# Local attention's output projection as three matmuls of split operands, with single buffers for two middle tiles

## The reference

```python
def attn_layer(x, Wqkv, qs, ksc, Wo):          # 16 heads of 64, INNER = 1024
    q, k, v = jnp.split(x @ Wqkv, 3, -1)        # x has its second half of channels shifted by a row
    q, k = rotary(l2norm(q) * qs), rotary(l2norm(k) * ksc)
    out = local_attention(q, k, v)              # windows of 64 rows, each looks at itself and the one before
    return out.transpose(0, 2, 1, 3).reshape(b, n, INNER) @ Wo
def ffn_layer(x, g, bln, W1, b1, W2, b2):
    a, gate = jnp.split(layer_norm(x) @ W1 + b1, 2, -1)
    return a * gelu(gate) @ W2 + b2
```

## Time and profile before

| | us |
|---|---|
| median of 3 runs | 2143.72 |
| range of the runs | 2138.83 to 2144.59 |
| profiled execution | 2145.24 |
| its span, first to last instruction | 2143.4 |
| PE / DVE / ACT / POOL busy | 2040.7 / 1723.7 / 1392.7 / 550.3 |

### The profile page before, as it was taken

One profiled execution on the slowest core, in us unless ns is written; L12 is line 12 of the kernel. 1 busy time (PEld: TensorE's weight loads), 2 busy tenths in 40 slices (PEclk: granted clock), 3 DMA queues, 4 the chain that ended last, 5 costly groups with the idle time before them and its releaser, 6 DMA issues.

```text
span 2143.4 us, 51804 instructions
## 1 busy us (share of the span) xinstructions
PE 2040.7 (95%) x17400; PEld 1704.1 (80%) x17400; DVE 1723.7 (80%) x4874; ACT 1392.7 (65%) x4026; POOL 550.3 (26%) x317
## 2 busy tenths in 40 slices
PE   5999999999998998999999999999999999999988
PEld 4787887887886676888888888888888888888877
DVE  6786787787676498898889888898889888988883
ACT  3776567567564355676767676866777676767653
POOL 2111111111111334232323233232323242323220
PEclk9999999999999999999999999999999999999999
DMA  3000000000000410021102011201120111011010
GB/s 120 8 10 1 7 12 1 7 12 1 6 26 0 140 31 15 13 72 33 56 14 72 14 58 31 72 14 46 44 73 14 34 57 52 25 33 55 14 33 20
DMA packets 50017, 72.10 MB, mean 34 GB/s; under 512 B 9429, under 2 KB 36869, under 8 KB 49541
## 3 DMA queue, kind: packets, MB, share of 16 engines
q1 hardware_dynamic: 47429, 64.30, 9.9%
q10 hardware_dynamic: 2368, 4.98, 0.6%
HBM read 51.58 MB, written 2.10 MB: 25 GB/s over the span
## 4 chain that ended last, share of the span: by engine, by line
PE 47%; issue 7%; DVE 4%; DMA 3%; ACT 3%; POOL 2%; SPq 1%; DVEq 0%; ACTq 0%; POOLq 0%
PE ps_loc L1722 17%; PE ps_loc L1830 7%; PE ps_loc L1799 5%; PE ps_loc L1761 4%; PE ps_loc L1841 4%; PE ps_loc L1772 4%; DMA late<-y_all 3%; PE ps_loc L1741 3%; PE ps_loc L1788 3%; POOL rnorm L2655 2%; PE ps_loc L1342 1%; ACT xnT_high L2077 1%; ACT pT L2060 1%; ACT xnT_loc L2077 1%; DVE w_low L2259 0%
## 5 line engine op out<-in xcount | busy, mean ns | idle before, releaser
L2655 POOL TENSOR_TENSOR rnorm<-norm_floor,half_loc 128x32 f32<-128x32 f32 x48 | 300.5, 6261 | 582.7 <-DVE norm_floor L2270 385.2
L1722 PE MATMUL ps_loc<-w_high,xT 128*128 128x512 f32 x1152 | 379.3, 410 | 0.7 <-ACT qk L2032 0.6
L2053 ACT ACTIVATE prob_loc<-prob_loc,top_loc 128x128 f32<-128x128 f32 x768 | 299.2, 402 | 45.2 <-DVE top_loc L2334 43.2
L718 ACT ACTIVATE prob<-prob,new_top 128x256 f32<-128x256 f32 x512 | 252.2, 497 | 0.0
L1722 PEld LDWEIGHTS ps_loc<-w_high,xT 128*128 128x128 f32 x1152 | 203.9, 189 | 51.4 <-issue 9.3
L2334 DVE CUSTOM_DVE_ANT_0 prob_loc<-ps_loc,const,rnorm 128x128 f32<-128x128 f32 x768 | 218.8, 345 | 28.0 <-PE ps_loc L1761 25.8
L1722 PE MATMUL ps_loc<-w_low,xT 128*128 128x512 f32 x576 | 228.5, 397 | 0.0
L2045 ACT ACTIVATE qT_loc<-ps_loc 128x512 f32<-128x512 f32 x96 | 57.4, 598 | 238.1 <-PE ps_loc L1741 238.1
L923 DVE CUSTOM_DVE_ANT_0 prob<-ps_cross,bias 128x256 f32<-128x256 f32 x512 | 184.7, 420 | 20.7 <-PE ps_cross L494 11.1
L1799 PE MATMUL ps_loc<-wo,qT_loc 128*128 128x256 f32 x768 | 169.8, 379 | 1.3 <-ACT qT_loc L2067 1.3
L1179 POOL TENSOR_TENSOR o<-o,alpha 128x1024 f32<-128x1024 f32 x32 | 61.0, 1906 | 425.1 <-DVE o L962 333.4
(11 more groups left out here) (214 smaller groups left out, 4869.0 us busy)
## 6 DMA issues: line engine op xcount, KB each, us to landing
w_raw<-in_ffn_Wqkv_dram SPq DMA_DIRECT2D x24, 512.0 KB, 5.7
w_raw<-in_ffn_Wqkv_dram SPq DMA_DIRECT2D x24, 256.0 KB, 3.9
wo<-in_ffn_Wo_dram SPq DMA_DIRECT2D x24, 256.0 KB, 3.5
v_mid<-v_even SPq DMA_DIRECT2D x24, 256.0 KB, 3.4
v_mid<-v_odd SPq DMA_DIRECT2D x24, 256.0 KB, 3.7
w<-in_ffn_W_dram SPq DMA_DIRECT2D x12, 341.0 KB, 3.3
w<-in_ffn_W_dram SPq DMA_DIRECT2D x6, 640.0 KB, 4.6
ctx_raw<-in_ctx_dram SPq DMA_DIRECT2D x12, 256.0 KB, 2.8
```

The source lines that it names most:

```text
L718: ins = act.activation(prob[:, t, h, :], prob[:, t, h, :], ACT.Exp, bias=new_top[:, t, h:h + 1], scale=-1.0, accum_out=chunk_sum[:, t, h:h ...
L1722: ins = pe.matmul(ps[:, DENSE + j % 2, :], xT[:, px, kk, t * P:(t + 1) * P], wqkv[pw][:, kk, col:col + 512], start=kk == 0 and n == 0, sto ...
L2053: ins = act.activation(pr, pr, ACT.Exp, bias=top[:, h, t:t + 1], scale=-1.0, accum_out=total[:, h, t:t + 1])
L2655: pool.tensor_tensor(rnorm[:, b % 2, t, :], norm2_floor[:, :], half[:, :], ALU.pow).then_inc(rnorm_done, 8)
```

## The change

Both operands of the projection are split into a high and a low part. ACT now writes all four groups of `oT_high`, DVE subtracts to get `oT_low` (`o_low`), and PE sums three products. Wo is split too: in slot 0 of each layer, ACT copies the high part right behind `q_out` (`out_weights_high`), and POOL subtracts the low one. Space comes from three places: `oT_low` lies over four of the six pairs of the probabilities' ring (so the next slot's third pair of scores waits for `y_full`), `v_mid` has one buffer, filled once the slot before has used it up, and `late` has one. In DVE's slot, `gated` 4 and 5 now stand ahead of the cosines.

```diff
-        self.wo = self.sb("wo", [P, PAIRS, D])
+        with ExitStack() as shared:
+            self.wo = self.sb("wo", [P, PAIRS, D], F32, shared)
+        self.wo_low = self.sb("wo_low", [P, PAIRS, D], F32R)
+        self.wo_high = self.sb("wo_high", [P, PAIRS, D], F32R)
...
+    LOW_RING = RING - PAIRS // 2
-        v_mid = sb("v_mid", [P, 2, INNER])
+        v_mid = sb("v_mid", [P, INNER])
-        late = sb("late", [P, B * TT, P])
+        late = sb("late", [P, TT, P])
...
             def shift(L, b):
                 sp.wait_ge(y_mid, L + U * (b + 1))
+                hold(sp, k.held)
+                sp.wait_ge(xn_done, L + U * b)
...
             def middle(L, b):
                 sp.wait_ge(qkv_done, L + U * (b + 1))
+                hold(sp, k.held)
+                sp.wait_ge(o_full, L + U * b)
...
             def project_out(a, b):
                 if b == 0:
-                    pe.wait_ge(wo_in, a + LAYER)
+                    pe.wait_ge(wo_split_low, a + LAYER)
                 pe.wait_ge(s_read, a + U)
                 pe.wait_ge(o_done, a + U)
                 for t in range(TT):
-                    for pair in range(PAIRS):
-                        ins = pe.matmul(ps[:, WIDE_OUT, t * D:(t + 1) * D], oT[:, pair, t * P:(t + 1) * P], wo[:, pair, :],
-                                        start=pair == 0, stop=pair == PAIRS - 1)
+                    for n, (po, pw) in enumerate(WIDE_PARTS):
+                        for pair in range(PAIRS):
+                            ins = pe.matmul(ps[:, WIDE_OUT, t * D:(t + 1) * D], oT[po][:, pair, t * P:(t + 1) * P],
+                                            wo_parts[pw][:, pair, :], start=n + pair == 0,
+                                            stop=n + pair == len(WIDE_PARTS) + PAIRS - 2)
...
+            def out_weights_high(L):
+                act.wait_ge(wo_in, L + LAYER)
+                for h in range(4):
+                    two = slice(2 * h, 2 * h + 2)
+                    act.activation(wo_parts[HIGH][:, two, :], wo[:, two, :], ACT.Copy).then_inc(wo_split_high, LAYER // 4)
...
                 q_out(a)
+                if b == 0:
+                    out_weights_high(L)
                 exps(a, 0)
...
                 probs_out(a, 4)
+                o_out(a, 1)
...
                     gates(f, 1)
+                o_out(a, 2)
...
+                if pair == LOW_RING:
+                    dve.wait_ge(y_full, a)
...
+            def o_low(a, g):
+                two = slice(2 * g, 2 * g + 2)
+                dve.wait_ge(o_high, a + 4 * (g + 1))
+                dve.tensor_tensor(oT[LOW][:, two, :], ps[:, OUT, :].rearrange("p (i t) -> p i t", i=2), oT[HIGH][:, two, :],
+                                  ALU.subtract).then_inc(o_done, 4)
...
+            def out_weights_low(L):
+                for h in range(4):
+                    two = slice(2 * h, 2 * h + 2)
+                    pool.wait_ge(wo_split_high, L + (h + 1) * (LAYER // 4))
+                    pool.tensor_tensor(wo_parts[LOW][:, two, :], wo[:, two, :], wo_parts[HIGH][:, two, :], ALU.subtract)\
+                        .then_inc(wo_split_low, LAYER // 4)
```

More of the change, by code:

```diff
@@ L136 @@
                 "q_done", "k_done", "s_full", "s_read", "exp_done", "rtotal_done", "p_done", "pT_full", "pT_done", "o_full",
-                "o_done", "y_full", "y_mid", "bn_done", "ln_stats", "ln_var", "ln_rstd", "xn_done", "xnT_full", "xnT_done",
+                "wo_high", "wo_low", "o_high", "o_done", "y_full", "y_mid", "bn_done", "ln_stats", "ln_var", "ln_rstd", "xn_done", "xnT_full", "xnT_done",
                 "w1_high", "w1_low", "xnT_high", "f_full", "gate_done", "u_done", "f2_full", "b2_done", "y_out")
@@ L1547, in local_layers @@
         v = (v_even, sb("v_odd", [P, TT, INNER]))
-        prob = sb("prob_loc", [P, 2 * RING, TT, P])
+        with ExitStack() as shared:
+            prob = k.sb("prob_loc", [P, 2 * RING, TT, P], F32, shared)
+        sb("prob_first", [P, 2 * LOW_RING, TT, P])
+        oT_low = sb("oT_low", [P, PAIRS, T], F32R)
         pT = sb("pT", [P, 2, 2, TT, P])
@@ L1556, in local_layers @@
         gate = sb("gate", [P, 2, T])
-        qT = k.sb("qT_loc", [P, PAIRS, T], F32, ctx, "right")
+        with ExitStack() as shared:
+            qT = k.sb("qT_loc", [P, PAIRS, T], F32, shared, "right")
+        oT_high = k.sb("oT_high", [P, PAIRS, T], F32R, ctx, "right")
         kT = k.sb("kT_loc", [P, PAIRS, T], F32, ctx, "right")
-        oT, uT = qT, kT
+        oT, uT = (oT_high, oT_low), kT
+        wo_parts = (k.wo_high, k.wo_low)
         DENSE, WIDE_OUT, FFN_OUT, TURN, OUT = 0, 2, 3, 6, 7
@@ L1582, in local_layers @@
          rnorm_done, twist_done, cos_done, sum_done, rope_done, q_cos_done, q_rope_done, qk_full, q_done, k_done, s_full, s_read,
-         exp_done, rtotal_done, p_done, pT_full, pT_done, o_full, o_done, y_full, y_mid, bn_done, ln_stats, ln_var,
+         exp_done, rtotal_done, p_done, pT_full, pT_done, o_full, wo_split_high, wo_split_low, o_high, o_done, y_full, y_mid, bn_done, ln_stats, ln_var,
          ln_rstd, xn_done, xnT_full, xnT_done, w1_split_high, w1_split_low, xnT_copied, f_full, gate_done, u_done, f2_full, b2_done,
@@ L1587, in local_layers @@
         mid_in = [sem(f"mid_in{n}") for n in range(2)]
-        late_in = [sem(f"late_in{b}") for b in range(B)]
+        late_in = sem("late_in")
         x_sum, out_done = sem("x_sum"), sem("out_done")
@@ L1783, in out @@
                     at = (pair % 2) * T
-                    for values, t, q0, q1 in ((v[b % 2][:, 0, :], 0, 0, P), (v_mid[:, b % 2, :], 1, 0, WINDOW),
+                    for values, t, q0, q1 in ((v[b % 2][:, 0, :], 0, 0, P), (v_mid, 1, 0, WINDOW),
                                               (v[b % 2][:, 1, :], 1, WINDOW, P)):
@@ L2066, in o_out @@
                 act.wait_ge(o_full, a + 4 * (g + 1))
[L2067 to L2068 removed]
+                act.activation(oT[HIGH][:, 2 * g:2 * g + 2, :], ps[:, OUT, :].rearrange("p (i t) -> p i t", i=2), ACT.Copy)\
+                    .then_inc(o_high, 4)
+            def out_weights_high(L):
[3 more added lines that the diff above has]
+                    act.activation(wo_parts[HIGH][:, two, :], wo[:, two, :], ACT.Copy).then_inc(wo_split_high, LAYER // 4)
             def xn_out(a, L, b):
@@ L2364, in halves @@
             def halves(b, t, last):
-                return (k.y[:, b * TT + t, 0:P], ps[:, TURN, t * P:(t + 1) * P] if last else late[:, b * TT + t, :])
+                return (k.y[:, b * TT + t, 0:P], ps[:, TURN, t * P:(t + 1) * P] if last else late[:, t, :])
             def moments(a, b, shifts, last=False):
@@ L2511, in slot @@
                     twists(n, nL, 1, 1)
+                o_low(a, 3)
+                if ahead:
                     norms(n, 1)
-                    cosines(n, 1, 1)
-                    sums(n, 1)
-                    cosines(n, 1, 0)
                 if ffn:
@@ L2519, in slot @@
                 if ahead:
+                    cosines(n, 1, 1)
+                    sums(n, 1)
+                    cosines(n, 1, 0)
                     q_sum(n, 1)
@@ L2681, in layer @@
                     norm(L - U, last_i, B - 1)
+                out_weights_low(L)
                 rotate(L + U, 1)
```

24 lines of the change are left out of this document (10 added, 14 removed).

## The result

| | before | after |
|---|---|---|
| median, us | 2143.69 (2138.83 to 2144.59) | 2233.2 (2231.81 to 2235.69) |
| ratio, 95% interval | | 1.0416 (1.0403 to 1.0428) |
| span of the profiled execution | 2143.4 | 2230.9 |

What follows compares the result with a forecast made beforehand. PE was taken as the bound, with ACT and DVE close behind. 0 + 7 + 47 + 19.5 + 6 - 1.2 = 78.3 us on 2145.24 gave 2223.5, expected as 2222, range 2165 to 2255.

Steps and rivals of the forecast that it cites:

- Slot 0: Start of slot 0, layers 1 to 5: ACT waits for Wo's load; PE 7.7 us late plus 1.7 for clock, 47 us.
- The matmuls and the chain: Ordinary slots: PE saves 1.24 us on the projection, the ACT and DVE chain takes it back; costed at 0.
- Slot 2: Slot 2, layers 0 to 4: ACT waits for the late v part of Wqkv; 3.9 us each, 19.5 us.
- Slot 3: Start of slot 3, layers 0 to 4: late `y_mid` delays filling `late`, so `moments` wait; 1.2 us each, 6 us.
- Starts of slots 1 and 2: `y_mid` 1.8 us later, so `late` fills later and `moments` wait; 0.6 us a slot, 12 slots, 7 us.
- Layer 0 slot 0: Wo is there since the start and the copies fit into ACT's wait for the first minima; 0 us.
- The last slot: End of the kernel, where no chain follows: the matmuls' saving stays, -1.2 us.
- Rival (d): Worse: POOL's subtractions of Wo meet DVE in its tight stretch; + 5 us in five layers, 2248; 12%.
- Rival (a): The chain has slack and the matmul saving survives, slot 0 and slot 2 costs stay; 2181, or 2180; 22%.

## Why the prediction was right

**Slot 0: the path right, the landing time with luck.** The path is the stated one, and PE went on at 16.5 us. Of the 9.4 a slot, 7.7 for the stall was 7.7 on average. The 1.7 for the clock was 2.2: I took it as partly covered by ACT, and the slots' lengths show none of it covered. Without Wo's copies at that place 35 of the 49 us go. But two terms of the landing were wrong and cancelled. In layer 1 SP began with Wo 4.5 us into the slot where it had been 3.6, so `y_mid` delayed it by 0.9 and not 1.8. And from its first issue to ACT's start Wo took 1027.33 - 1020.94 = 6.4 us, where I had 5.2.

**The matmuls and the chain: right.** 5.67 us, `widen` 4 later by 1.3 (forecast 1.1 to 1.2), ordinary slots unchanged. The wait at `widen` 4 is 0.6 and not about 1. The run without subtractions shows the chain as the cause: 0.6 to 1.2 us a slot comes back, 0.9 on average.

**Slot 2: mechanism right, term too small** (3.9, measured 5.1 a layer). DVE's tail behind `gated` 5 was taken as 7.8 us and is 8.7: three weight subtractions took 2.39 and `scaled_keys` 1.47. `narrow` started 0.3 later than forecast in layer 1 besides. I had the tail's new length in the sum; the two runs on single buffers and on the gates' order show how much hangs on it: 1 us with the old order and old projection, 4 to 5 with the new. A kernel with the old order in slot 2 alone was not tried.

**Slot 3: 1.7 a layer, not 1.2.** `moments` ran at 10.2 us into the slot, forecast 10.0. The slot remained at 58.0 with the v part early, because `y_mid` still came 1.3 us after the start. With the weight subtractions behind `add_attention` it comes 0.85 before the start and the slot takes 57.4 to 57.7. There PE's wait of 1.20 us for `add_ffn` is what the traces show of the last microsecond.

**Starts of slots 1 and 2: wrong, 0 and not 7.** The step that failed is `y_mid`'s distance to the slot's start. I had 0.2 us before it; it is 55.47 - 54.33 = 1.1 in slot 1. The chain ahead of `norms` grew by the full 1.8, but I let POOL's 6.30 us follow unchanged, and it took 5.43. `moments` ran at 7.8 to 7.9 in most of these slots where I had 8.6, inside the slack.

**Layer 0 slot 0: 3.4, not 0.** The copies did fit into ACT's wait for the first minima. What I left out is POOL behind them: its subtractions met DVE, and in the first 18 us PE waits 2.5 us where it waited 1.1. With Wo's copies later, the wait of 1.53 is gone. Later in the slot, without a feed-forward to cover `o_low`, PE's waits grow by another 0.9 (2.09 us at L1804 and 1.64 at L1816 for `o_low`, where it waited 1.92 and 1.25 for copies). The shorter projection gives back 1.24. The mean granted clock of the slot fell from 0.95 to 0.90, some 3 us, which is more than the 2.3 that are left. The last slot's 2.1 us stay unexplained. Between the kernels of this study it varies from 73.3 to 78.2 us.

**Rival (d)** had a right mechanism, which costs little in the changed kernel. In layer 1 the subtractions of Wo ran from 1037.5 to 1042.5, while DVE computed minima from PSUM; only in layer 0 did they meet DVE. As soon as the stall is repaired, they meet it in every layer, for 1.4 to 2.8 us in the slots shown. Rival (a), that the saving survives, is excluded by the ordinary slots.

## What to carry to other kernels

A step in the queue of an engine that others wait for should not wait for a DMA that was timed for a later reader: where a load's first reader moves ahead by 25 us, the load has to move too. When operands are split to make matmuls cheaper, count the subtraction on the engine that makes them: of 1.24 us saved on PE here, about 0.9 went back on a path that had 0.1 us of slack. And repairing a stall moves work onto other work, so read the durations again after each repair, not only the waits.
